# Reordering VectorE's queue in an expert layer / attention / expert layer kernel

## The reference

```python
x = x + 0.5 * ffn(layernorm(x), gate_weight, gate_up_proj, down_proj)
x = x + attn(layernorm(x), Wq, Wk, Wv, Wo)       # 16 heads of 16, 4 KV heads, rope, softmax over 1024 keys
x = x + 0.5 * ffn(layernorm(x), gate_weight, gate_up_proj, down_proj)
# ffn: 32 experts, inner width 96; all are computed:
#   out += (silu(x @ g.T) * (x @ u.T)) @ d.T * combine[:, e]
# combine: softmax of the router's logits, top 8, kept up to a cumulative share of 0.8, renormalised
```

## Time and profile before

| what | value |
| --- | --- |
| time, median of 3 runs (lowest to highest) | 2312.97 us (2312.69 to 2313.44) |
| time of the profiled execution | 2313.61 us |
| span from its first to its last instruction | 2311.8 us |
| PE busy | 2240.8 us, 97% |
| DVE busy | 1581.2 us, 68% |
| ACT busy | 1242.3 us, 54% |
| POOL busy | 1063.5 us, 46% |
| granted TensorE clock, mean | 0.999 |

### The profile page before, as it was taken

One profiled execution on the slowest core, in us unless ns is written; L12 is line 12 of the kernel. 1 busy time (PEld: TensorE's weight loads), 2 busy tenths in 40 slices (PEclk: granted clock), 3 DMA queues, 4 the chain that ended last, 5 costly groups with the idle time before them and its releaser, 6 DMA issues.

```text
span 2311.8 us, 48013 instructions
## 1 busy us (share of the span) xinstructions
PE 2240.8 (97%) x19280; PEld 1498.7 (65%) x19280; DVE 1581.2 (68%) x3138; ACT 1242.3 (54%) x1973; POOL 1063.5 (46%) x864
## 2 busy tenths in 40 slices
PE   2999999999999999999999999999999999999998
PEld 2888875555565565565556555665655655688887
DVE  7766579877877877877777876676777753454543
ACT  4433331666666666566666566666656666533332
POOL 1866653443443443443434434333433434465665
PEclk9999999999999999999999999999999999999999
DMA  5210121011101011100110111010010010011010
GB/s 214 74 39 24 39 57 30 17 28 31 30 17 50 20 37 25 30 23 20 44 30 22 25 32 31 11 41 14 19 42 11 15 36 10 21 29 30 19 39 19
DMA packets 111878, 77.78 MB, mean 34 GB/s; under 512 B 57508, under 2 KB 103844, under 8 KB 110888
## 3 DMA queue, kind: packets, MB, share of 16 engines
q1 hardware_dynamic: 111512, 74.69, 11.7%
q10 hardware_dynamic: 144, 0.03, 0.0%
HBM read 62.87 MB, written 11.80 MB: 32 GB/s over the span
## 4 chain that ended last, share of the span: by engine, by line
PE 90%; DVE 7%; issue 1%; POOL 1%; ACT 0%; DMA 0%; POOLq 0%; DVEq 0%; ACTq 0%
PE PS L1128 42%; PE PS L1146 21%; PE PS L1158 11%; PE PS L1191 11%; DVE arena L912 1%; PE PS L1170 1%; PE PS L1110 1%; PE PS L1087 1%; PE PS L1232 1%; DVE XN L792 1%; PE PS L1218 1%; DVE turned L875 0%; POOL arena L543 0%; DVE arena L889 0%; DVE arena L897 0%
## 5 line engine op out<-in xcount | busy, mean ns | idle before, releaser
L1128 PE MATMUL PS<-XT,WGU 128*128 128x256 f16 x9216 | 1116.1, 274 | 37.3 <-DVE WGU L758 20.8
L1128 PEld LDWEIGHTS PS<-XT,WGU 128*128 128x128 f16 x9216 | 875.8, 98 | 262.1 <-issue 133.0
L548 POOL TENSOR_TENSOR arena<-arena 128x512 f16<-128x512 f32 x384 | 450.3, 1173 | 1139.0 <-ACT arena L624 1138.9
L912 DVE TENSOR_REDUCE arena<-PS 128x1 f32<-128x512 f32 x1024 | 657.5, 684 | 344.8 <-PE PS L1158 342.3
L647 ACT ACTIVATE arena<-PS,fac 128x512 f32<-128x512 f32 x1024 | 646.2, 684 | 240.4 <-PE PS L1170 239.2
L617 ACT ACTIVATE arena<-PS,fac 128x512 f32<-128x512 f32 x384 | 263.9, 687 | 706.4 <-PE PS L1128 706.3
L1146 PE MATMUL PS<-WD,arena 128*128 128x256 f16 x4608 | 569.2, 273 | 6.7 <-DVE X L904 4.7
L1146 PEld LDWEIGHTS PS<-WD,arena 128*128 128x128 f16 x4608 | 431.7, 98 | 149.5 <-issue 91.5
L543 POOL TENSOR_TENSOR arena<-arena 128x512 f32<-128x512 f32 x384 | 501.1, 1305 | 45.8 <-DVE arena L897 36.6
L889 DVE SCALAR_TENSOR_TENSOR arena<-arena,PS 128x512 f32<-128x512 f32 x384 | 260.9, 679 | 270.9 <-ACT arena L617 270.0
L1158 PE MATMUL PS<-arena 48*128 48x512 f16 x1024 | 312.6, 382 | 3.3 <-DVE arena L912 2.4
(11 more groups left out here) (116 smaller groups left out, 793.1 us busy)
## 6 DMA issues: line engine op xcount, KB each, us to landing
arena<-ce_scratch SPq DMA_DIRECT2D x256, 128.0 KB, 3.2
arena<-wgu SPq DMA_DIRECT2D x4, 1536.0 KB, 13.0
arena<-q_scratch SPq DMA_DIRECT2D x192, 32.0 KB
arena<-ktab_c SPq DMA_DIRECT2D x16, 256.0 KB, 4.0
q_scratch<-arena SPq DMA_DIRECT2D x32, 128.0 KB, 1.7
out<-X SPq DMA_DIRECT2D x8, 512.0 KB, 3.0
X<-wd SPq DMA_DIRECT2D x2, 1536.0 KB, 23.0
X<-x SPq DMA_DIRECT2D x1, 3072.0 KB, 11.4
```

Source lines behind the costliest of these rows:

```text
L548: pool.tensor_tensor(hs[1][:, d % HS, :], tw[d % 2], hs[0][:, d % HS, :], ALU.subtract).then_inc(lo_done, 1)
L912: dve.tensor_reduce(mx[:, half * REP * QT + c:half * REP * QT + c + 1], PS[:, B_MAX + half, :], AX_X, ALU.max).then_inc(max_taken, 1)
L1128: ins = pe.matmul(PS[:, b, j * HALF_G:(j + 1) * HALF_G], WGU[w][:, kt, part * CHUNKS + c + j, :], XT[r][:, k % 2, kt, half * HALF_G:(half ...
```

## The change

Everything but the order of work stays. The third join of a group moves from slot 12 to slot 14, and with it its rope sum (15), its split (16) and its store (17). For `k` from 1 to 8 the four norm steps of the next group move from slots 9, 10, 11, 12 to 6, 7, 9, 11, the inverse root from 10 to 8, and the split of the rows from 13 to 12; other groups keep their slots. `load(2)` and the earliest slot of the later loads move by two slots. `max_rows` leaves the visit: behind a slot's first visit it now comes after `gated` and `product`; behind the second, in a slot of three visits, after the slot's second event and before the third visit; behind the last visit of a slot, at the slot's very end, after its norm step and its first event. Two event slots change by the move: in `k=7` slot 12 `out_T` becomes the first event, and in slot 14 of `k=4` and `k=6` `tok_T` and `out_T` become second ones.

```diff
-P_HI, P_LO, P_JOIN, T_HI, T_LO, T_LOGITS = 6, 7, 8, 15, 16, 17
+P_HI, P_LO, T_HI, T_LO, T_LOGITS = 6, 7, 15, 16, 17
+JOIN_AT = (8, 10, 14)
+NORM_AT, ALONE_AT = ((6, 7, 9, 11), 8, 12), ((9, 10, 11, 12), 10, 13)
...
-                at[k * PER_GROUP + P_JOIN + 2 * j].append(("join", k - 1, j))
+                at[k * PER_GROUP + JOIN_AT[j]].append(("join", k - 1, j))
...
+def steps_of_norm(k):
+    return NORM_AT if 1 <= k <= GROUPS else ALONE_AT
...
-                    if s in (11, 13, 15):
-                        store_block(k - 1, s // 2 - 5)
+                    if s - 3 in JOIN_AT:
+                        store_block(k - 1, JOIN_AT.index(s - 3))
...
-                if d == FIRST:
+                if d == FIRST + 2:
                     load(2)
...
-                    if u >= QKV and d == max(SLOT_OF[FILLS * (u - QKV) + FILLS] + 1, 2 * PER_GROUP * (u // KV + 1) + 16):
+                    if u >= QKV and d == max(SLOT_OF[FILLS * (u - QKV) + FILLS] + 1, 2 * PER_GROUP * (u // KV + 1) + 18):
...
-                if 1 <= k <= GROUPS and s in (10, 12, 14):
-                    rope_low(k - 1, s // 2 - 5)
+                if 1 <= k <= GROUPS and s - 2 in JOIN_AT:
+                    rope_low(k - 1, JOIN_AT.index(s - 2))
...
-                    if s == 10:
+                    if s == steps_of_norm(k)[1]:
                         inverse_roots(norm_of_group(k + 1))
-                    if s == 13:
+                    if s == steps_of_norm(k)[2]:
                         rows_low(norm_of_group(k + 1))
...
                 if f < VISITS:
                     maximum(f)
-                    if f % FILLS == FILLS - 1:
-                        max_rows(f // FILLS)
+            def unit_ends(v):
+                f = v + AHEAD
+                if f < VISITS and f % FILLS == FILLS - 1:
+                    max_rows(f // FILLS)
...
                     product(d + 1)
-                if 1 <= k <= GROUPS and s in (9, 11, 13):
-                    rope_sum(k - 1, (s - 9) // 2)
+                if (d, 0) in VISIT:
+                    unit_ends(VISIT[d, 0])
+                if 1 <= k <= GROUPS and s - 1 in JOIN_AT:
+                    rope_sum(k - 1, JOIN_AT.index(s - 1))
...
                 if (d, 2) in VISIT:
+                    unit_ends(VISIT[d, 1])
                     visit(VISIT[d, 2])
...
-                    if 9 <= s < 13:
-                        norm_of(k + 1, s - 9)
+                    if s in steps_of_norm(k)[0]:
+                        norm_of(k + 1, steps_of_norm(k)[0].index(s))
...
                     event(d, 0)
+                if (d, 2) in VISIT:
+                    unit_ends(VISIT[d, 2])
+                elif (d, 1) in VISIT:
+                    unit_ends(VISIT[d, 1])
```

More of the change, by code:

```diff
@@ L711, in _ @@
                         rows_high(norm_of_join(k - 1))
-                    if s in (10, 12, 14):
-                        rope_high(k - 1, s // 2 - 5)
+                    if s - 2 in JOIN_AT:
+                        rope_high(k - 1, JOIN_AT.index(s - 2))
                 if 0 <= k < PREPS - 1:
-                    if s == 13:
+                    if s == steps_of_norm(k)[2]:
                         rows_high(norm_of_group(k + 1))
```

## The result

| | before | after |
| --- | --- | --- |
| time, median of 6 runs (lowest to highest) | 2313.08 us (2312.69 to 2314.36) | 2303.38 us (2302.56 to 2304.08) |
| profiled execution | 2313.61 us | 2302.74 us |
| its span | 2311.8 us | 2300.9 us |

The ratio is 0.9957, with a 95% interval from 0.9944 to 0.9970: 9.7 us faster, where 10.2 were forecast, at 2303.38 us for 2302.8.

What follows compares the result with a forecast made beforehand. PE, busy 97%, was taken to bound the kernel, its waits released by DVE. 4.7 + 1.7 + 2.73 + 2.58 - 1.5 = 10.2 us off the 2312.97 us median gave 2302.8 us, range 2298.5 to 2310.

Steps and rivals of the forecast that it cites:

- The dense sum and its clock: Slots 12 and 13, k=1 and 2: PE's dense-sum waits vanish, 4.7 us; k=2's clock fall goes, 1.7 us.
- rival B: k=1 and 2: stretched norm step in slot 11 stalls PE, clock falls; gives back 6.4 us, 2309.2 us; chance 0.14.
- Slot 13: k=3 to 8: up projections wait 4.14 us for the join; 1.41 stays at slot 15, gain 2.73 us.
- The rule of even visits: Slot 15, k=3, 5 and 8: an even visit, lacking the values' matmuls, leaves PE waiting 0.47 us each.
- The moved steps: Next group's norm steps in their new slots: DVE's slack covers most, cost 1.5 us for all eight groups.
- rival D: Slot 7: norm step 1 stretches behind POOL's row split, join 0 late; 2318.3 us at full price; chance 0.08.
- D's own sign: PE waits for a join's bank (L877) in slot 9 above 1.2 us.
- max_rows: Waits before k=7's gate projection, 1.85 us, and k=9 slot 17's out_y, 0.73 us, vanish: together 2.58 us.
- the other ends of units are priced at nothing: Unit ends other than those in k=7 slot 6 and k=9 slot 17: waits too short to count, zero gain.
- Rival C: Waits for attention outputs shrink as DVE has fewer steps in slots 9 to 12: 2.7 us more, 2300.1; chance 0.08.

## Why the prediction was right

The sum of 10.2 us met 9.7 in the medians (10.9 in the profiled executions); its terms less closely. Measured by slots:

- **The dense sum and its clock**, 4.7 + 1.7 forecast. The slots 11 to 14 are together 2.7 us shorter in `k=1` and 4.4 in `k=2`, 7.1 for 6.4. Of the difference 0.2 us in each group is a short wait in slot 11, behind join 1, that left with the norm steps (the kernel with the join alone still has it); the other 0.3 has no row of its own. That the stall is a queue is shown by the two single kernels: either move takes away part, 1.5 and 0.4 us a piece are left.
- **The stall one slot on**, rival B, did not come: at 2.32 us step 3 fits. How near it was shows in the kernel with the doubled step: there the gate projection waits 2.46 us in `k=1`, and in `k=2` the clock falls too.
- **Slot 13**, 2.73 forecast. With the join alone slots 12 to 15 of `k` = 3 to 8 give 2.7 us, as forecast. With the norm steps moved too they give 3.4 (without the 0.5 us of `k=8`, which the next point counts). The rule of even visits held to the digit, 0.47 three times, and again with the join in slot 13. What is above the forecast lies in slot 13 of `k=5` (0.3) and `k=7` (0.4) and went with the norm steps, where the kernel with the join alone has waits of up to 0.24 us.
- **The moved steps**, 1.5 forecast: 0.5, all in slot 12 of `k=8`, where an output stands behind step 3 and the gate projection waits for it. Their price was probably kept down by the instructions' own times, which no run separates: the longest L810 is now 1.22 us for 2.30, the median 0.17 for 0.72, though rival D put it behind POOL's row split. D's own sign stayed away, as no wait for a join was above 1.2 us:

```profile
L800 DVE TENSOR_SCALAR XN<-X,mv,rstd x96: 397/403/1355, 11.3 to 2158.5; 128x256 f32<-128x256 f32 x96
...
L810 DVE TENSOR_SCALAR var<-mv x24: 169/170/1216, 8.2 to 2149.0; 128x4 f32<-128x4 f32 x24
```

- **max_rows**, 2.58 forecast: this term was mis-sized. The step that failed is "the other ends of units are priced at nothing". Behind events it brought more than I had counted: 2.0 us in `k=7`, 0.9 in `k=4` slot 21 and 0.9 in slot 12 of `k=8`. The last two are waits for an `out_y` that I had not looked for, though they lay within the 4.6 us of the earlier trace rows. Behind the product it cost 2.2, 1.2 and 0.6 us and gained four times 0.2, 3.2 net, and in `k=9` slot 17 the wait only changed from `out_y` to the maxima. Rival C saw the waits for `out_y` shrink, and they did, from 4.6 to 1.6 us, but by this move and not by the steps: with joins and norm steps alone they are 5.1. Net 0.6 us gained, which agrees with the 0.2 us between the kernels with and without the move as far as runs can tell.

So the right total is partly luck: one term 2 us too high, three together 2.4 us too low. And the reading that would have caught it was in my own text: L920 took 1.72 us because POOL was at work, a finding that I used for the norm steps and not for the four instructions that the change itself put behind `product`, the instruction that sets POOL going.

## What to carry to other kernels

In a hand-ordered queue ask of each moved instruction what the other engines do at that moment: in this kernel the place behind the instruction that releases POOL was the worst of three for short SBUF work on DVE, and ahead of `gated` the best. Two moves that empty the same slot are not worth their sum; test each alone, since one part may bring nearly all. And work moved into slack should be tried doubled: here it fitted with some 0.5 us to spare in `k=1` and 2, which its price of 0.5 us did not show.

## What the runs showed of the hardware

**DVE held by POOL.** In the changed kernel the four instructions of `max_rows` take 0.9 us with POOL idle and up to 4.2 us behind the product, and each stretched one ends within 0.1 us of POOL's. With `weigh` kept away (between gated and product) one is stretched and ends with `low`; in `k=6` a second one ends with the split of the block, POOL's L538. The Trainium skill, GPSIMD Engine Reference, § Key points, has GpSimd share its SBUF interfaces with VectorE, in contention with instructions in a two-port mode or with two SBUF inputs. The trace agrees for L928 and L930, which have two SBUF inputs; L929 and L810 have one and were stretched too, and no view names their mode. The trace also shows the size: the stretch lasted as long as POOL's instruction did, so it looks like a hold and not like a slower rate. `product`, `gated` and the maxima, which read PSUM, kept their 0.69, 0.68 and 0.68 us beside POOL throughout, and L804, with one SBUF input, never took more than 0.43.

**The clock.** After an idle PE of 2.3 us the granted clock fell to the lower level (1.2 GHz) in `k=2` before and in the kernel with `max_rows` alone, not in `k=1` of either (means of 0.58 and 0.68 against 1.00); after 1.5 us (the join alone) it fell in neither. The doubled step shows it in `k=2` and, after its longest wait of 3.17 us, in `k=5`, and again not in `k=1`, whose wait was the same 2.46 us as that of `k=2`. Length of the wait alone does not decide; what does, these runs leave open.
